# Building the blur's band matrices during the mixing stage's last steps instead of at the start of the tail stage

## What is computed

```python
def layer0(v):                                   # v = _gn(x): 32 groups of 4 channels
    ll, lh, hl, hh = haar_dwt(v)                 # 512 channels of 128 x 128
    h = gelu(batchnorm(conv1x1(concat(ll, lh, hl, hh), w_c1, b_c1), bn1_g, bn1_b))
    o = dwconv3x3(h, dw_w, dw_b)
    o = layernorm_chw(o, gn_g, gn_b)             # over C, H, W of one image
    u = conv1x1(gelu(conv1x1(o, pw1_w, pw1_b)), pw2_w, pw2_b) + h
    g = gelu(batchnorm(conv1x1(u, w_c2, b_c2), bn2_g, bn2_b))
    return haar_idwt(*split(g, 4))
y = x + layer0(_gn(x))
out = y + depthwise_conv4x4(_gn(y), flip(kernel), pad=(2, 1))   # the same 4 x 4 kernel for every channel
```

## Time and profile before

| | us |
|---|---|
| median of 3 runs | 5690.55 |
| lowest and highest of them | 5673.53, 5690.85 |
| the profiled execution | 5687.8 |
| its span, first to last instruction | 5685.9 |
| mixing stage starts (first instruction) | 1235.6 |
| tail stage starts | 2583.4 |
| first unit's convolution starts | 2610.06 |

### The profile page before, as it was taken

How to read it: one execution, slowest core, us unless ns; L and a number is a source line. 1 busy time by engine, 2 the same in 40 slices (tenths; PEclk the granted TensorE clock), 3 DMA queues, 4 the chain that set the end, 5 groups by cost and what they waited for, 6 DMA issues and landing times. The chain is left out here.

```text
span 5685.9 us, 67157 instructions
## 1 busy us (share of the span) xinstructions
PE 5206.1 (92%) x18136; PEld 3152.4 (55%) x18136; DVE 4380.2 (77%) x5325; ACT 3721.4 (65%) x5012; POOL 2068.4 (36%) x1397
## 2 busy tenths in 40 slices
PE   2888888986999999996689999999999999999999
PEld 1333333332555555563256666666666766666677
DVE  8555555428999999957988888888888888888833
ACT  0333333346778777754678788787887877878744
POOL 0000000028777777730023333333333333333354
PEclk9999999998999999998899999999999999999999
DMA  9999999842333333326999999999999999999986
GB/s 368 374 372 380 369 380 378 345 143 71 108 108 112 104 108 108 108 83 226 326 381 403 393 401 398 390 402 384 398 392 384 394 384 397 399 384 395 400 292 228
DMA packets 829594, 1729.83 MB, mean 304 GB/s; under 512 B 50064, under 2 KB 587152, under 8 KB 718608
## 3 DMA queue, kind: packets, MB, share of 16 engines
q1 hardware_dynamic: 755472, 1389.81, 66.9%
q10 hardware_dynamic: 73728, 335.58, 14.4%
HBM read 1050.95 MB, written 674.23 MB: 303 GB/s over the span
## 5 line engine op out<-in xcount | busy, mean ns | idle before, releaser
L1080 POOL TENSOR_TENSOR y_lo<-y_centred_tile,y_hi 128x1024 fp32r<-128x1024 f32 x512 | 1042.3, 2057 | 1728.4 <-ACT y_centred_tile L1416 1422.9
L1295 PE MATMUL blur_psum<-y_hi,band_hi 128*128 128x512 f32 x4096 | 1129.3, 417 | 8.9 <-DVE y_tile L1173 7.4
L1278 PE MATMUL conv_psum<-u_in,w_conv 128*128 128x512 f32 x2048 | 975.3, 620 | 106.2 <-DVE pair_sums L1151 81.2
L1295 PE MATMUL blur_psum<-y_lo,band_hi 128*128 128x512 f32 x4096 | 1041.8, 396 | 6.7 <-POOL y_lo L1080 6.3
L1295 PEld LDWEIGHTS blur_psum<-y_hi,band_hi 128*128 128x128 f32 x4096 | 765.8, 188 | 278.8 <-issue 100.6
L1151 DVE TENSOR_TENSOR pair_sums<-gelu_out,conv_psum 128x512 f32<-128x512 f32 x1024 | 653.1, 683 | 308.7 <-ACT conv_psum L1386 308.6
L1295 PEld LDWEIGHTS blur_psum<-y_lo,band_hi 128*128 128x128 f32 x4096 | 769.7, 188 | 199.4 <-POOL y_lo L1080 14.8
L1173 DVE SCALAR_TENSOR_TENSOR y_tile<-blur_psum,rstd_all,y_tile 128x1024 f32<-128x1024 f32 x512 | 639.4, 1276 | 160.5 <-PE blur_psum L1295 153.1
L1386 ACT ACTIVATE gelu_out<-conv_psum,bn_shift,bn_scale 128x512 f32<-128x512 f32 x512 | 397.5, 776 | 534.1 <-PE conv_psum L1278 512.7
L1278 PEld LDWEIGHTS conv_psum<-u_in,w_conv 128*128 128x128 f32 x2048 | 399.4, 198 | 559.7 <-issue 406.2
L601 POOL TENSOR_TENSOR tap_products<-tap_products 128x512 f32<-128x512 f32 x512 | 653.5, 1276 | 42.7 <-ACT tap_products L838 6.2
(11 more groups left out here) (168 smaller groups left out, 5445.2 us busy)
## 6 DMA issues: line engine op xcount, KB each, us to landing
x_tile<-x SPq DMA_DIRECT2D x256, 1024.0 KB, 10.1
y_scratch<-x_tile ACTq DMA_DIRECT2D x256, 1024.0 KB, 8.4
y_tile<-y_scratch SPq DMA_DIRECT2D x512, 512.0 KB, 10.9
out<-y_tile SPq DMA_DIRECT2D x512, 512.0 KB, 10.4
x_stream<-x SPq DMA_DIRECT2D x192, 1024.0 KB, 11.6
x_resident<-x SPq DMA_DIRECT2D x160, 1024.0 KB, 11.0
z_scratch<-z_tile ACTq DMA_DIRECT2D x256, 256.0 KB, 7.2
z_in<-z_scratch SPq DMA_DIRECT2D x256, 256.0 KB, 3.6
```

The source lines that it names most:

```text
L1080: nc.gpsimd.tensor_tensor(y_lo[:, h, part, 2:2 + W], y_c[:, part, :], y_hi[:, h, part, 2:2 + W].bitcast(F32), ALU.subtract).then_inc(s_lo, 1)
L1278: nc.tensor.matmul(cv[s][:], w[:, s * C:(s + 1) * C], u_t[:, k % US, :], start=True, stop=True).then_inc(s_mm, 1)
L1295: ins = nc.tensor.matmul(bl[t][:, 2 * c:2 * c + 2, :], wt[:, kw, :], y[:, h, ch:ch + 2, kw:kw + W], start=(m == 0 and kw == 0), stop=(m == ...
```

## The change

- The band matrices move from the tail's preamble to the mixing stage. `band_hi`, `band_lo` and their seam versions are now keepers. One kernel column kw is built after the residual of each of the pieces l = 240 to 243 (`band_column`, 8 instructions), and the split follows after the residual of piece 244 (`band_parts`, 4 instructions). The unsplit matrices lie in `tap_products`, which nobody uses any more at that point.
- The count of the rests (line 1137 before) stays in the preamble.
- To make room, `z_in` has three slots instead of four, so the load of piece e waits for `gelu_first` of piece e - 3, and `o_stats` has no buffer of its own but lies over `z_sum`, which has been read by then.
- PE waits for the second convolution's weights ahead of the third product instead of the first.

```diff
@@ -97,7 +97,9 @@
...
         gram = sbk("gram", [128, C + 1])
-        keepers.update(K=K, n128=n128, quarter=quarter, gram=gram)
+        bands = [sbk(name, [rows, 4, cols], F32R) for name, rows, cols in (
+            ("band_hi", 128, 128), ("band_lo", 128, 128), ("seam_band_hi", 96, 48), ("seam_band_lo", 96, 48))]
+        keepers.update(K=K, n128=n128, quarter=quarter, gram=gram, bands=bands)
         phase_mix(nc, keepers, pw1, pw2, const, z_d, u_d)
@@ -434,6 +436,7 @@
...
 AHEAD = 2
+Z_SLOTS = 3
@@ -446,7 +449,7 @@
...
         o_buf = sb("depthwise_out", [128, O_SLOTS, BANK])
-        z_in = sb("z_in", [128, 4, BANK])
+        z_in = sb("z_in", [128, Z_SLOTS, BANK])
         diag = sb("tap_diagonals", [128, PE_TAPS, C])
@@ -455,13 +458,17 @@
...
         u_tr = sb("u_transposed", [128, 2, 4, C + 1])
-        bst = sb("o_stats", [128, STEPS, BN_W])
+        bst = kp["z_sum"][:, 0:STEPS * BN_W].rearrange("p (a b) -> p a b", b=BN_W)
         mv = sb("o_mean_var", [128, 2])
...
         b1 = sb("pw1_bias", [128, 2])
+        band_hi, band_lo, sband_hi, sband_lo = kp["bands"]
+        KR = kp["KR"]
+        band = products[:, 0, 0, :].rearrange("p (k m) -> p k m", m=128)
+        sband = products[0:96, 0, 1, 0:192].rearrange("p (k m) -> p k m", m=48)
         dw_p = [ps(f"dw_psum{i}", [128, BANK]) for i in range(2)]
@@ -479,7 +486,7 @@
...
         s_bn1 = sem("bn1_ready")
-        s_z = [sem(f"z_loaded{i}") for i in range(4)]
+        s_z = [sem(f"z_loaded{i}") for i in range(Z_SLOTS)]
         s_h = sem("h_rows_ready")
@@ -539,10 +546,10 @@
...
             def load(e):
-                if e >= 4:
-                    sp.wait_ge(s_h, e - 3)
+                if e >= Z_SLOTS:
+                    sp.wait_ge(s_h, e - Z_SLOTS + 1)
                 b, j = divmod(e, STEPS)
-                sp.dma_start(z_in[:, e % 4, :], zv[b, :, j * BANK:(j + 1) * BANK]).then_inc(s_z[e % 4], 16)
+                sp.dma_start(z_in[:, e % Z_SLOTS, :], zv[b, :, j * BANK:(j + 1) * BANK]).then_inc(s_z[e % Z_SLOTS], 16)
@@ -662,7 +669,7 @@
...
                 nc.vector.memset(waiter[:], 0.0)
-                ln.link(nc.vector.bn_aggr(mv[:], bst[:].rearrange("p a b -> p (a b)")))
+                ln.link(nc.vector.bn_aggr(mv[:], kp["z_sum"][:, 0:STEPS * BN_W]))
                 ln.link(nc.vector.tensor_tensor(t[:, 0:1], mv[:, 0:1], V[:, V_DWB:V_DWB + 1], ALU.add))
@@ -693,6 +700,25 @@
...
                 dve.wait_ge(s_gacc, b + 1)
+
+            def band_column(kw):
+
+                for kh in range(4):
+                    for to, first, cols in ((band, K_TM, 128), (sband, K_SM, 48)):
+                        rows = 96 if to is sband else 128
+                        mask = K[0:rows, first + kh * cols:first + (kh + 1) * cols]
+                        scalar = KR[0:rows, kh * 4 + kw:kh * 4 + kw + 1]
+                        if kh == 0:
+                            lk.link(nc.vector.tensor_scalar(to[:, kw, :], mask, scalar, None, ALU.mult))
+                        else:
+                            lk.link(nc.vector.scalar_tensor_tensor(to[:, kw, :], mask, scalar, to[:, kw, :],
+                                                                   ALU.mult, ALU.add))
+
+            def band_parts():
+                lk.link(nc.vector.tensor_copy(band_hi[:], band))
+                lk.link(nc.vector.tensor_copy(sband_hi[:], sband))
+                lk.link(nc.vector.tensor_tensor(band_lo[:], band, band_hi[:].bitcast(F32), ALU.subtract))
+                lk.link(nc.vector.tensor_tensor(sband_lo[:], sband, sband_hi[:].bitcast(F32), ALU.subtract))
@@ -714,6 +740,11 @@
...
                     norm_columns(b - 1)
+
+                if l >= ALL2 - 16 and l < ALL2 - 12:
+                    band_column(l - (ALL2 - 16))
+                if l == ALL2 - 12:
+                    band_parts()
@@ -795,12 +826,12 @@
...
             def gelu_first(e):
-                act.wait_ge(s_z[e % 4], 16 * (e // 4 + 1))
+                act.wait_ge(s_z[e % Z_SLOTS], 16 * (e // Z_SLOTS + 1))
                 at = block_of(e)
...
                     act.wait_ge(s_u, last + 1)
-                rows = z_in[:, e % 4, :].rearrange("p (r c) -> p r c", c=W2)
+                rows = z_in[:, e % Z_SLOTS, :].rearrange("p (r c) -> p r c", c=W2)
                 if at % BLOCKS == BLOCKS - 1:
@@ -903,12 +934,7 @@
...
         junk = sb("junk3", [128, XW], BF16)
-        band = sb("band", [128, 4, 128])
-        band_hi = sb("band_hi", [128, 4, 128], F32R)
-        band_lo = sb("band_lo", [128, 4, 128], F32R)
-        sband = sb("seam_band", [96, 4, 48])
-        sband_hi = sb("seam_band_hi", [96, 4, 48], F32R)
-        sband_lo = sb("seam_band_lo", [96, 4, 48], F32R)
+        band_hi, band_lo, sband_hi, sband_lo = kp["bands"]
         y_t = sb("y_tile", [128, YS, 2, GRP, W])
@@ -1119,21 +1145,6 @@
...
-            for kw in range(4):
-                for kh in range(4):
-                    for to, first, cols in ((band, K_TM, 128), (sband, K_SM, 48)):
-                        rows = 96 if to is sband else 128
-                        mask = K[0:rows, first + kh * cols:first + (kh + 1) * cols]
-                        scalar = KR[0:rows, kh * 4 + kw:kh * 4 + kw + 1]
-                        if kh == 0:
-                            lk.link(nc.vector.tensor_scalar(to[:, kw, :], mask, scalar, None, ALU.mult))
-                        else:
-                            lk.link(nc.vector.scalar_tensor_tensor(to[:, kw, :], mask, scalar, to[:, kw, :],
-                                                                   ALU.mult, ALU.add))
-            lk.link(nc.vector.tensor_copy(band_hi[:], band[:]))
-            lk.link(nc.vector.tensor_copy(sband_hi[:], sband[:]))
-            lk.link(nc.vector.tensor_tensor(band_lo[:], band[:], band_hi[:].bitcast(F32), ALU.subtract))
-            lk.link(nc.vector.tensor_tensor(sband_lo[:], sband[:], sband_hi[:].bitcast(F32), ALU.subtract))
             nc.vector.tensor_scalar(d_t[:, 4 * C:8 * C], band_lo[:].bitcast(F32).rearrange("p k m -> p (k m)"), 0.0, None,
@@ -1240,11 +1251,11 @@
...
         def _(pe):
-            pe.wait_ge(s_w, 16)
             pe.wait_ge(s_v, 1)
...
             nc.tensor.matmul(cv[1][:, 0:C], mean_row[:], mean_row[:], start=True, stop=True).then_inc(s_p, 1)
+            pe.wait_ge(s_w, 16)
             pe.wait_ge(s_v, 3)
```

## The result

| | before | after |
|---|---|---|
| median of the runs, us | 5690.7 (10 runs, 5673.53 to 5697.34) | 5667.18 (10 runs, 5661.09 to 5683.55) |
| ratio of after to before | | 0.9967 (95%: 0.9955 to 0.9978) |
| profiled execution / its span, us | 5687.8 / 5685.9 | 5670.85 / 5669.0 |

The ratio of 0.9967 is 18.8 us less (12.5 to 25.6); the two medians themselves lie 23.5 us apart. The forecast was 13.65 us less, a ratio of 0.9976. The forecast time was 5677, and 5667.18 lies inside the range. The two profiled executions differ by 16.95 us. The question of this study is therefore twofold: whether the 13.65 us are made up as the sum says, and where the rest comes from, 3 us by the traces and 5 by the ratio.

A forecast was written before the change was run, and what follows sets the result against it. PE was taken to bound drain and most of the tail, DVE image 0, with a serial preamble stretch between; -1.9 - 12.05 + 0.3 + 0 = -13.65 us gave about 5677 us, range 5660 to 5691.

The forecast's parts named there:

- the sum: Whole kernel: weights' wait -1.9, bands -12.05, drain +0.3, three slots 0, together -13.65 us.
- The wait for the weights: Tail's preamble: PE's first product starts 1.9 us earlier, the weights landing 0.2 us before the third product asks; bounds 0 and 1.9.
- The bands off the preamble: Tail's preamble: without the band instructions line 1140 starts 12.05 us earlier, POOL's power being the next late input.
- The drain: Mixing stage's last steps: four band columns make DVE late by 1.44 us against 1.24 slack, costing 0.3 us; bounds 0 and 1.44.
- The ring of three: Mixing stage: three `z_in` slots cost 0 us, in steady steps and at the start; bounds 0 and 2.1.
- The clock stays up: Rival, preamble: shorter PE idleness keeps the clock at 2.4 GHz, at most 2.8 us less, 5674 us; chance 0.10.
- The head start is swallowed: Rival, tail: queueing image 0 loads or a stalling PE branch eat the earlier start, in the extreme 5690 us; chance 0.10.
- Three slots are too few: Rival, mixing stage: z loads come late and lose 42 us over 85 rounds, giving 5719 us; chance 0.06.
- The runs' own spread: Rival, whole kernel: runs fall mostly where the one low run before did, median 5660 us; chance 0.12.
- B4: Theory set up after the measurement for the gain beyond the sum: the clock made something beside the preamble faster; no size given.
- neither is fed from the outside by anything with a fixed time: Tail: DVE paces image 0 and PE the rest, so the stages behind the preamble are shifted whole.

The follow-up runs named there:

- bands twice: The changed kernel with the 36 band instructions also repeated in the tail's preamble, on a scratch buffer; median 5677.26 us, ratio 0.9983.
- bands only: The changed kernel with PE's wait for the weights put back ahead of the first product; median 5675.34 us, ratio 0.9974.
- old places of y: The changed kernel with a 2816-byte hole ahead of `y_tile`, putting it and what follows back where they lay before; median 5675.22 us, ratio 0.996.
- mixing stage's places only: The changed kernel with the band instructions taken out of the drain and built in the preamble alone; median 5683.03 us, ratio 0.9983.
- wait only: The kernel before with only PE's wait for the second convolution's weights moved to the third product; median 5689.36 us, ratio 1.0.
- ring of three only: The kernel before with only three `z_in` slots and `o_stats` laid over `z_sum`; median 5692.07 us, ratio 1.0009.
- tail's places only: The kernel before with only the tail's buffers placed as in the changed kernel, bands still built in the preamble; median 5693.58 us, ratio 0.9998.
- the count in the drain: The changed kernel with count, its product and cast also in the drain, columns over eight steps; median 5706.9 us, with 14 filler words 5688.03; also run with 62.

## Why the prediction was right, and where it was not

**The wait for the weights** was forecast at 1.9 us, on the reading that the weights land 0.2 us before the third product asks for them. That step failed: in the changed kernel, and in the nine others with the wait moved, the landing still releases the third product. In the changed kernel it waits 0.47 us, but DVE's `u_covariance` ends only at 2589.18 and would have let it go 0.06 us later, so the landing costs 0.08 us there; in the kernel with the wait alone moved it costs 0.86. The third product started 2588.17 - 2583.39 = 4.78 us after the weights' issue before and 2589.32 - 2586.57 = 2.75 after, so the term is 2.03. Its size was nearly met because errors cancel. The forecast put that start 4.78 - 1.9 = 2.88 us after the issue. The first product came 0.28 us later than forecast (1.05 us after the issue, not 0.77, as DVE's own first operations came later), the landing added 0.08, and 0.50 us was won because the first two products ran before the clock fell: 0.38 us and 0.48, against 0.57 and 0.79. The row of the second product before, which the earlier trace rows leaves out:

```profile
2587.00 0.79 PE L1247 MATMUL conv_psum<-u_mean_row 1*128 1x128 f32 x2 [0.37 <-DVE u_mean_row L1109]
```

Since the landing takes 2.67 to 3.25 us from execution to execution, pairs of single executions give 1.57 (before against the wait alone) and 2.50 (15.03 - 12.53).

**The bands off the preamble**: forecast 12.05 with POOL's power next late. From the third product to the scale were 2608.20 - 2588.17 = 20.03 us before and 2597.28 - 2589.32 = 7.96 after: 12.07. POOL releases the scale, as forecast. From the scale to the convolution 1.86 became 1.82. In sum 2.03 + 12.07 + 0.04 = 14.14, against 13.95.

**The drain**: forecast 0.3, measured 0.05. The mis-sized term is DVE's step with a column, summed as 0.75 + 2.66 = 3.41 us; it takes 3.31 or 3.32. The column itself takes its 2.66 us here too (2545.36 - 2542.70), but it starts at 2542.70, 0.09 us before the residual's row ends (2542.04 + 0.75), so only 0.66 of the residual's 0.75 us count. (The expectation of the run with two columns a step took this difference for a shorter column, 2.56 us.) DVE is 0.26 to 0.27 late per column, 1.07 after four, under the slack of 1.24, and PE is hardly touched. The slack of 1.24 itself was a sound reading: with two columns in a step PE waits for `u_tile` at once.

**The ring of three**: forecast 0, bounds 0 and 2.1; the one wait, at the start, is 0.35 us against 0.71. Nothing in the steady steps.

**The rivals.** *The clock stays up*: no. The granted clock was 0.98 up to 2589 us and the first two products took 0.86 us instead of 1.36, but from 2589 to 2592 it was 0.50 and the third took 2.07 as before. What the upper level gave is this 0.5 us, not 2.8. *The head start is swallowed*: no. Image 0 takes 232.8 us against 233.3, and a preamble of 12.2 us more costs 9.1 us by the ratio. Nor does the branch stall: from the cast to the convolution are 2599.10 - 2597.75 = 1.35 us, 1.39 before. *Three slots are too few*: no. *The runs' own spread*: the ten runs of before have their median at 5690.7, where the first three had it. On the chances: 0.68 stood on a change within 0.3% (17.1 us) and 0.26 on a larger gain. The measured 18.8 us lie just past that bound, on the side given 0.26, and their interval (12.5 to 25.6) holds both.

**What the sum does not hold.** Beyond the preamble, the traces differ by another 2.8 us (16.95 - 14.14), the runs by about 5 (18.8 - 14.1). One part is seen: in image 1 the third unit takes 11.68 us before and 9.89 after. There the granted clock stays at its lower level of 1.2 GHz over the whole unit in one kernel and not in the other. Windows of the kernel with only the tail's buffers moved, whose preamble is that of before (its third unit lies from 2857.5 to 2869.2), and of the changed kernel (2847.0 to 2856.9):

```profile
2851.30:2857.50 6.20, 2.33 (x5) 1.30 (x6) 5.96 (x13) 2.09 (x2) 0.00 (x0) 0.50 1.02 334
2857.50:2869.20 11.70, 7.97 (x15) 3.25 (x14) 8.16 (x16) 5.16 (x7) 0.55 (x1) 0.50 1.00 354
```
```profile
2841.50:2847.00 5.50, 2.29 (x5) 1.25 (x6) 5.29 (x11) 2.31 (x3) 0.00 (x0) 0.81 0.85 274
2847.00:2856.90 9.90, 5.86 (x15) 2.43 (x14) 8.15 (x15) 5.16 (x7) 0.55 (x1) 0.84 1.05 405
```

The same 15 products take 7.97 us of PE's time in the one and 5.86 in the other. The Trainium skill (TensorE: Matmul & The Clock Gate, part 1) has activity release the faster level; the rows agree as far as the low level comes in and just behind image 0, where PE is busy 144.24 of 226 us, and is gone from 3200 to 5200 us, where it is busy 1971.31 of 2000. Where the level rises goes in part with where image 1 begins: with preambles of 26.7 to 27.0 us the third unit took 11.68 to 11.69 in all three kernels, with 12.4 to 25.1 us 9.89 in all eight. It is no simple order: of the three kernels with about 9.8 us two took 11.50 and 11.57 and one 9.89, and with the bands built twice the fourth and sixth units took 1.6 us more each (10.93 and 11.13 against 9.34 and 9.57), so that its image 1 took 345.0; with the old places of `y_tile` they did so too (10.84 and 11.13). This is worth 1.8 us here, was in no term of the sum, and is luck of the timing.

The rest stays open. By the ratios, each kernel with the bands kept across the mixing stage gains 3 to 9 us more than its preamble is shorter:

```
kernel                    gain by the ratio, us   preamble shorter by, us   left over
changed                          18.8                    14.1                 4.7
bands twice                       9.7                     1.9                 7.8
bands only                       14.8                    11.6                 3.2
old places of y                  22.8                    14.3                 8.5
mixing stage's places only        9.7                     2.1                 7.6
wait only                         0.0                     1.6                -1.6
ring of three only               -5.1                    -0.4                -4.7
tail's places only                1.1                     0.0                 1.1
```

The last three do not have these buffers, and what is left over in them is small or a loss. Taken singly, only two of the upper five have an interval that excludes their own preamble's gain: the bands twice (4.6 to 14.8 us) and the mixing stage's places only (4.0 to 14.8). No stretch of the traces holds the surplus: images 2 to 7 lie between 2185.7 and 2199.8 us in the upper five and 2189.5 and 2195.5 in the lower three, and the untouched stage ahead of the mixing varies from 1230.8 to 1245.0 us between single executions. B4, the clock, is not excluded either. The recorded mean clocks of the runs were 0.9707 with the mixing stage's places only, against 0.9689 for the runs of the kernel before beside them. With two levels, 0.0018 of 5690 us is 20 us less at the lower level, of which the preamble holds 2. In every kernel with six or more runs the slower runs had the lower clock, and in the fourteen traces the untouched first stage is longer where more of it lies at the lower level (1230.8 us with a mean clock of 0.94, 1245.0 with 0.93). But it does not fit in order: the bands twice had 0.9697 against 0.9690, the wait only 0.9696 against the same, with 7.8 and -1.6 us left over. Which is cause and which goes with it, no run tells. The surplus is shown by the runs, near their resolution (an interval is some 5 to 9 us to either side); its cause is not.

**What was wrong in the reading of the tail.** The prediction held that DVE paces image 0 and PE the rest, "and neither is fed from the outside by anything with a fixed time". For this change it did no harm, as the loads' demands moved with the work. But from image 3 on the transfers are a bound beside PE: the DMA share stays at 1.05 with every placement, and where a packet of the x loads takes 4% longer (326.3 to 339.6 ns), an image takes 2.3% longer (366.5 to 375.1 us). The row with 1.04 stood in the earlier trace rows; I used it only for the rival and should have named the transfers a second bound. In the kernels with the count in the drain this cost more than the 2.7 us that they won. None of the kernels run here is faster than the changed one by more than the intervals.

## What to carry to other kernels

Work on a serial stretch between two stages was worth its full length here, within the intervals, and a neighbouring stage's engine took it for nothing up to the slack of its handover to the bound engine; read that slack from one step's rows and spread the work so that the sum of the overruns stays under it. When a wait is moved later, ask what the waiter does next: the same landing may still release it, and the gain is then the work that slips in front of it. Before a kernel whose DMA share is at its ceiling gets another small buffer, look at the addresses of the transfers' buffers: here every kernel with them at multiples of 256 bytes was among the fast ones.

## What the runs showed of the hardware

- With a DMA share of 1.05, the place of the SBUF buffers matters: moving all of the tail's by 32 bytes, from a multiple of 256, raised the mean 8192-byte packet of the loads into `x_tile` from 326.3 to 339.6 ns and left that of the stores from it at 310.1 and 310.2; the wait of PE for `u_in` rose from 1.5 to 23.4 us in 2000, and the execution by 52.5 us (5669.0 to 5721.5, one execution each). At a multiple of 64 an image took 6 to 7 us more than in the changed kernel, at the one of 128 about 2, in kernels that also have the count in the drain.
- In ten kernels the first small product behind 1.61 to 1.88 us of PE idleness took 0.38 us; in four, behind 3.51 to 4.02 us, it took 0.45 to 0.59. The third product took 2.07 or 2.08 us in twelve of the fourteen, whichever the first took; in the other two it took 1.73 and 1.98. In the drain, waits of 1.67 and 2.69 us in two neighbouring steps were enough for the clock to fall to 0.65 in the next step, in which PE was busy 4.81 of 4.81 us.
- The eight dependent small operations of a column took DVE 2.66 us in the preamble and in the drain alike, from the first one's start to that of the next instruction. A small operation behind a residual starts 0.09 us before the residual's row of 0.75 us ends, so the rows' lengths do not add up to the step.
- The same load of 256 KB, issued first at the tail's start, landed after 2.67 to 3.25 us in the fourteen traces.
